# A post-norm layer on one core: scores in 32x32 tiles, |Kh| on ScalarE, Newton in one piece, new orders on every engine

## The reference, cut to what matters

```python
# x: (16, 256, 128); 16 heads of 8; window 128; FFN 128 -> 352 -> 128, fp4 in blocks of 16
g, v = x @ Wg.T + bg, x @ Wv.T + bv                       # per head
corr = dot(g_i, g_j) / (|g_i||g_j| + 1e-8), masked to j <= i and j >= i - 128
corr = (corr + 1) / 2
denom = mean_j(corr) + 0.5
fitness = 1 / (denom * sum_i(1 / denom))
attn = softmax(corr * fitness_i, masked with -1e10)
x = layernorm(x + (attn @ v) @ Wo.T + bo)
h = silu(q4(x) @ q4(Wgate).T) * (q4(x) @ q4(Wup).T)
x = layernorm(x + q4(h) @ q4(Wdown).T)
# q4: s = max|block| / 6; round x/s to the grid 0, .5, 1, 1.5, 2, 3, 4, 6; times s
```

## Time and profile before

| | |
|---|---|
| median of 3 runs | 390.52 us (386.58 to 390.61) |
| the profiled execution | 388.84 us, of which the span from first to last instruction is 387.0 us |
| mean granted TensorE clock | 0.944 of full |
| busy: PE, DVE, ACT, POOL | 329.3, 285.6, 223.8, 188.2 us |
| PE's matmul instructions | 2964, and as many weight loads |

### The profile page before, as it was taken

How to read it: one execution, slowest core, us unless ns; L and a number is a source line. 1 busy time by engine, 2 the same in 40 slices (tenths; PEclk the granted TensorE clock), 3 DMA queues, 4 the chain that set the end, 5 groups by cost and what they waited for, 6 DMA issues and landing times.

```text
span 387.0 us, 8906 instructions
## 1 busy us (share of the span) xinstructions
PE 329.3 (85%) x2964; PEld 196.2 (51%) x2964; DVE 285.6 (74%) x820; ACT 223.8 (58%) x499; POOL 188.2 (49%) x466
## 2 busy tenths in 40 slices
PE   6368878798899999999999999999998999967542
PEld 4234444454455565655565555555554556635331
DVE  1535356667879797979797979797979798886751
ACT  2034564566667776767676767777776777513210
POOL 7754033507274747374737373737373333541441
PEclk9999998899999999999999999999999999985655
DMA  4001000000010101010101010100000000000000
GB/s 117 27 1 29 14 2 3 27 2 29 0 30 3 42 1 42 0 46 1 42 0 45 1 43 2 43 0 30 3 30 0 29 3 27 15 0 14 15 14 19
DMA packets 12405, 7.64 MB, mean 20 GB/s; under 512 B 1026, under 2 KB 12356, under 8 KB 12356
## 3 DMA queue, kind: packets, MB, share of 16 engines
q1 hardware_dynamic: 12356, 7.03, 6.4%
HBM read 4.93 MB, written 2.10 MB: 18 GB/s over the span
## 4 chain that ended last, share of the span: by engine, by line
PE 30%; DVE 23%; POOL 20%; issue 17%; ACT 8%; POOLq 0%; ACTq 0%; DVEq 0%
PE OT L745 6%; PE S L722 5%; PE WA L871 4%; POOL nt L463 4%; PE S L726 3%; ACT Pm L561 3%; POOL rstd L496 3%; POOL nt L465 3%; POOL rn L470 3%; POOL nt L468 2%; DVE A L1274 2%; POOL B L510 2%; DVE xn L1166 2%; PE WB L784 2%; DVE h L1118 2%
## 5 line engine op out<-in xcount | busy, mean ns | idle before, releaser
L561 ACT ACTIVATE Pm<-S 128x384 f32<-128x384 f32 x256 | 111.7, 490 | 64.0 <-PE S L726 63.9
L722 PE MATMUL S<-mask,ident 128*128 128x384 f16 x256 | 65.8, 340 | 10.0 <-ACT Pm L561 7.8
L745 PE MATMUL OT<-Pm,gv 128*32 128x256 f32 (+1 forms) x1024 | 56.8, 341 | 0.0
L487 POOL TENSOR_TENSOR hq<-hm,hs 128x352 f32<-128x352 f32 x32 | 25.2, 789 | 63.8 <-DVE hm L1136 63.6
L726 PE MATMUL S<-BT,AT 32*128 32x256 f16 (+1 forms) x512 | 44.3, 252 | 0.0
L745 PEld LDWEIGHTS OT<-Pm,gv 128*32 128x32 f32 x1024 | 27.2, 111 | 21.4 <-issue 6.0
L726 PEld LDWEIGHTS S<-BT,AT 32*128 32x128 f16 x512 | 14.4, 93 | 43.0 <-issue 43.0
L722 PEld LDWEIGHTS S<-mask,ident 128*128 128x128 f16 x256 | 18.9, 99 | 33.7 <-issue 14.8
L840 PE MATMUL WD<-wdT,hqT 128*128 128x128 f32 (+1 forms) x192 | 29.5, 311 | 1.5 <-ACT hqT L614 1.5
L840 PEld LDWEIGHTS WD<-wdT,hqT 128*128 128x128 f32 (+1 forms) x192 | 26.3, 217 | 4.1 <-ACT hqT L614 2.2
L1112 DVE SCALAR_TENSOR_TENSOR hh<-th,WC 128x352 f32<-128x352 f32 x29 | 15.0, 518 | 17.7 <-ACT th L585 17.6
(11 more groups left out here) (160 smaller groups left out, 724.4 us busy)
## 6 DMA issues: line engine op xcount, KB each, us to landing
xT<-x_turned_dram SPq DMA_DIRECT2D x16, 128.0 KB, 2.2
x_res<-x_dram SPq DMA_DIRECT2D x16, 128.0 KB, 2.1
out_dram<-yo SPq DMA_DIRECT2D x16, 128.0 KB, 2.1
wf<-w_down_dram SPq DMA_DIRECT2D x1, 176.0 KB, 2.6
wgv<-wgv_dram SPq DMA_DIRECT2D x1, 128.0 KB
wf<-w_gate_dram SPq DMA_DIRECT2D x1, 128.0 KB, 2.2
wf<-w_up_dram SPq DMA_DIRECT2D x1, 128.0 KB, 2.2
woT<-wo_dram SPq DMA_DIRECT2D x1, 64.0 KB
```

Of the source, the lines that this page charges most:

```text
L487: pool.tensor_tensor(b3(hq[:, k, 0:I]), b3(hm[:, k]), bc(hs[:, k], QB), ALU.mult).then_inc(s_hq, 1)
L561: act.activation(Pm[:, group % PR, hd % 4, :], S[:, (H * x + hd) % 3, 0:SCW], ACT.Exp, scale=1.0 / ZS).then_inc(s_exp, 1)
L722: pe.matmul(S[:, bank, 0:SCW], ident16[:, :], mask16[:, :], start=True, stop=False)
L745: i = pe.matmul(OT[VP * g:VP * (g + 1), T - (q1 - q0):T], gv_flat[:, at:at + VP], Pm[:, (GROUPS * x + c) % PR, g, q0:q1], start=(kt == 0 a ...
```

## The change

- `scores`: the two L726 matmuls of a head become eight of at most 32 keys by 32 contraction rows. For keys 0 to 127 each tile of 32 keys covers 160 queries, for keys 128 to 255 it covers 128, 96, 64 and 32. The mask is added last, by four matmuls of a 32x32 identity with 3 x 32 columns of mask16. What lies outside of these is set to MASKED in PSUM once, by nine DVE memsets ahead of everything (awaited by the first exponential).
- `round_h`: ScalarE computes hu = |2^22 * hn - 4| (`step_of_h`), GpSimd's hrn is negated, and DVE rounds by two scalar_tensor_tensor: (max(hu, ROUND) + hn), (max(hu, ROUND) - hm).
- GpSimd: all three Newton steps in one piece at the start of its step, then B's high part, then rstd of layer norm 1; h/scale of both halves behind A's high part.
- DVE: for t >= 0 the three `gene_size` instructions stand between the fitness instructions, ahead of gate and up; gh ahead of the h scales; B's low part behind the maxima of h; x's quantising ahead of A's low part; at t < B the reciprocal and the attention stay inside `quant_x`.
- ACT: gsq and gv ahead of `values_out(t, 0)` and the exponentials of pair 6; `step_of_h` around the copy of B.

```diff
 scores(x, p)
-                for hd, bank in pair:
-                    pe.matmul(S[:, bank, 0:SCW], ident16[:, :], mask16[:, :], start=True, stop=False)
-                for kt, (q0, q1) in enumerate(((0, T), (T, SCW))):
+                for kt in range(NT):
                     for hd, bank in pair:
                         r, c = 32 * (hd % 4), hd // 4
-                        i = pe.matmul(S[:, bank, q0:q1], AT[r:r + 32, x % 2, c, kt * P:(kt + 1) * P],
-                                      BT[r:r + 32, x % 2, c, T - (q1 - q0):T], start=False, stop=(kt == 1))
-                        if kt == 1:
-                            i.then_inc(s_sc, 1)
+                        for k0 in range(0, P, KG):
+                            at, n = (k0, P + KG) if kt == 0 else (T + k0, P - k0)
+                            q = kt * P + k0
+                            pe.matmul(S[k0:k0 + KG, bank, at:at + n], AT[r:r + 32, x % 2, c, q:q + KG],
+                                      BT[r:r + 32, x % 2, c, q:q + n], start=(kt == 0), stop=False)
+                near = mask16[:, :].rearrange("p (b c) -> p b c", c=P)
+                for n, (hd, bank) in enumerate(pair):
+                    m = 32 * (hd % 4)
+                    for k0 in range(0, P, KG):
+                        i = pe.matmul(S[k0:k0 + KG, bank, 0:SCW].rearrange("p (b c) -> p b c", c=P)[:, :, k0:k0 + KG],
+                                      ident16[m:m + KG, m:m + KG], near[m:m + KG, :, m:m + KG],
+                                      start=False, stop=True)
+                    i.then_inc(s_sc, 1)
...
 GpSimd's step
                 if live(t + 2):
-                    newton(t + 2, (0, 1, 2) if t < 0 else (0,))
-                if live(t - 2) and t != B + 1:
-                    rstd(t - 2, mv1, ve1, rstd1, nm1, nb1, s_ln1, 5 * (t - 2) + 5, s_rs1)
+                    newton(t + 2)
...
                     pool.tensor_copy(B16[:, :, 0:3:2, :], twice(Bf)).then_inc(s_Bhi, 1)
-                if live(t + 2) and t >= 0:
-                    newton(t + 2, (1, 2))
-                if live(t - 3):
-                    h_over_scale(t - 3, 0)
+                if live(t - 2) and t != B + 1:
+                    rstd(t - 2, mv1, ve1, rstd1, nm1, nb1, s_ln1, 5 * (t - 2) + 5, s_rs1)
...
 ScalarE
+            def step_of_h(x, k):
+                act.wait_ge(s_hn, NT * x + k + 1)
+                act.activation(hu[:, k], hn[:, k], ACT.Abs, bias=off[:, :], scale=STEP).then_inc(s_hu, 1)
...
 round_h(x, k, step), two steps in place of four
+                dve.scalar_tensor_tensor(out=hm[:, k], in0=hu[:, k], scalar=ROUND, in1=hm[:, k] if step else hn[:, k],
+                                         op0=ALU.max, op1=op).then_inc(s_hr, 1)
...
 VectorE, ahead of everything
+            for k0 in range(0, P, KG):
+                for a, b in ((0, k0), (k0 + P + KG, T), (T, T + k0)):
+                    if a < b:
+                        dve.memset(S[k0:k0 + KG, :, a:b], MASKED).then_inc(s_far, 1)
```

More of the change, by code:

```diff
@@ L32 @@
 MASKED = -60000.0
+KG = 32
 ZS = 256.0
@@ L397, in _ @@
             pool.memset(onesf[:, :], 1.0).then_inc(c_pool, 1)
+            pool.memset(off[:, :], STEP_OFF).then_inc(s_off, 1)
             for n in range(2):
@@ L450, in bias_rows, with newton @@
                 pool.wait_ge(c_pool, 30)
-            def newton(x, steps):
+            def newton(x):
                 y0 = rn[:, :]
@@ L456, in newton @@
                 sd = seed[:, :].bitcast(F32)
-                for k in steps:
+                for k in range(3):
                     src = sd if k == 0 else y0
@@ L578, in apply_1 @@
                 need(act, s_ln2, 5 * (t - 2 - YR) + 1)
-                need(act, s_xq, 9 * (t - 2 - YR) + 5)
+                need(act, s_xq, 9 * (t - 2 - YR) + 4)
                 ln_apply(y, rstd1, nb1, y1[:, (t - 2) % YR], s_y1)
@@ L655, in _ @@
                                    WA[:, :].rearrange("p (q d) -> p q d", d=HD), ACT.Copy).then_inc(s_gvc, 1)
+                if live(t):
+                    values_out(t, 0)
+                exps(t, 6)
                 if live(t - 2):
@@ L1106, in residual_2, with low_B @@
                                   WD[:, 0:T].rearrange("p (n d) -> p n d", n=NT), ALU.add).then_inc(s_ln2, 1)
+            def low_B(x):
+                dve.wait_ge(s_Bhi, x + 1)
+                need(dve, s_B, x)
+                dve.tensor_tensor(B16[:, :, 1:4:2, :], twice(Bf), B16[:, :, 0:3:2, :], ALU.subtract).then_inc(s_Blo, 1)
             def gate(x, k):
@@ L1219, in _ @@
                     ln_aggr(t - 4, s_ln2, st2, mv2)
+                if t < 0 and live(t + 1):
+                    low_B(t + 1)
                 if live(t - 3):
@@ L1223, in _ @@
                     up(t - 3, 1)
[L1225 to L1232, removed]
                 if live(t + 2):
@@ L1237, in _ @@
                     need(dve, s_Alo, t + 2)
+                    need(dve, s_fit, 8 * (t + 2))
                     dve.tensor_tensor(gh[:, :, :],
@@ L1244, in _ @@
                 if live(t - 3):
+                    h_scale(t - 3, 0)
+                if t >= 0 and live(t + 1):
+                    low_B(t + 1)
+                if live(t - 3):
+                    h_scale(t - 3, 1)
                     h_scale(t - 3, 2)
-                if t == B:
+                if live(t - 2) and t < B:
+                    for step in range(4):
+                        quant_x(t - 2, step)
+                if live(t - 1):
                     dve.wait_ge(s_ob, t)
@@ L1249, in _ @@
                     dve.reciprocal(orec[:, :], o[:, :, HD]).then_inc(s_on, 1)
+                if live(t - 2) and t < B:
+                    quant_x(t - 2, 4)
+                if live(t - 1):
                     dve.wait_ge(s_on, t)
@@ L1252, in _ @@
                     dve.tensor_tensor(attn[:, :, :], o[:, :, 0:HD], bc(orec[:, :], HD), ALU.mult).then_inc(s_attn, 1)
[L1253 to L1275 removed]
+                if t == B:
+                    for step in range(5):
+                        quant_x(t - 2, step)
+                if live(t - 2) and t <= B:
+                    quant_x(t - 2, 5)
                     quant_x(t - 2, 6)
@@ L1280, in _ @@
                     down_weights()
+                if live(t + 2):
+                    dve.wait_ge(s_Ahi, t + 3)
+                    need(dve, s_A, t + 2)
+                    dve.tensor_tensor(A16[:, :, 2:4, :], twice(gh), A16[:, :, 0:2, :], ALU.subtract).then_inc(s_Alo, 1)
                 if live(t - 3):
                     round_h(t - 3, 0, 0)
-                    round_h(t - 3, 0, 1)
-                    round_h(t - 3, 0, 2)
                 if live(t - 4) and t != B + 1:
@@ L1325, in _ @@
                     gate(t - 2, 0)
-                if live(t + 3) and t != -2:
-                    gene_size(t + 3, 0)
-                if live(t - 2):
                     up(t - 2, 0)
-                if live(t + 3) and t != -2:
-                    gene_size(t + 3, 1)
-                    gene_size(t + 3, 2)
+                if t in (-3, -1):
+                    for k in range(3):
+                        gene_size(t + 3, k)
                 if t == -3:
```

79 lines of the change are left out of this document (31 added, 48 removed).

## The result

The changed kernel takes 364.2 us (median of 4 runs, 361.29 to 365.56), the one before 390.27 in the same comparison: a ratio of 0.935 (0.928 to 0.942). The forecast was 354, with 342 to 373 for the range. The profiled execution took 365.38, of which the span is 363.5, against 388.84 and 387.0 before. So 23.5 us of span went, where 36.1 were forecast.

A forecast was written before the change was run, and what follows sets the result against it. PE's work and a ring through the engines both held the 19.26 us period; the ring would bind at 17.1. Savings of 21.6, 4.5, 6.5, 1.0 and 2.5 took 388.84 to 352.7, plus 1.7 gave 354; range 342 to 373.

The forecast's parts named there:

- Up to 99.99 ... 6.5: Start up to the steady stretch: 1.8 for step 0, 3 for steps 1 and 2, 2 for the fill, less 0.3 memset.
- granted clock falling in the middle because PE now idles: One of the listed signs that would show the forecast wrong; no size given.
- The pair: Score matmuls of two heads on PE: from 0.70 us to 0.43, between bounds of 0.35 and 1.52.
- A: Rival on the scores: small matmuls cost 20 ns each rather than 7, pair 0.66, total 371; chance 0.15.
- B: Rival on the scores: tiles of one head run one after another at 0.056, total 469, slower; chance 0.05.
- PE's work: PE's work per steady period: 18.75 us of 19.26 before, 16.3 after the change.
- The ring: Dependency loop through the engines in each steady period: 17.1 us after, 4.1 of PE and ACT plus 13.0 of DVE.
- Rounding: Rounding h on DVE: from 3.42 us to 1.76 per period, saving 1.66.
- The seed: Newton's seed, three DVE instructions now ahead of rden: adds 0.65 us to the ring.
- rival C: GpSimd's rstd of layer norm 1 comes late: one us per period, ring 18.1, total 364 to 366; chance 0.12.
- D: Rival on ACT: Abs needs another function table, four loads of 1.283 us, some 400 us; chance 0.04.
- Two further steps, last pairs, tail: Savings after the ten steady periods: 4.5 us for two steps, 1.0 for last pairs and rounding, 2.5 for the tail.

The follow-up runs named there:

- e1_warm: The changed kernel with idle-time matmuls ahead of pairs in steps 0 and 1 and ahead of step 2's turn of the weights: 356.93 us, ratio 0.919.
- e3_tiles_only: The kernel before with only the new 32x32 scores and their nine memsets: 401.26 us, ratio 1.033.
- e4_old_scores: The changed kernel with the old scores everywhere: 376.86 us, ratio 0.970.
- e7: e1_warm with the three gene_size (seed) instructions right behind rden instead of between the fitness instructions: 358.94 us.
- e9: e1_warm with layer norm 1's rstd between Newton steps two and three, its apply ahead of pair 2's exponentials, h maxima ahead of gh: 371.70 us, ratio 0.958.
- e10_fill_all: e1_warm with more idle-time matmuls, from the start through step 0 and in the gaps of the last steps: 352.68 us, ratio 0.908.
- e6: e1_warm with GpSimd's old order (rstd and B's high part after Newton step one) and the seed behind gate and up: 424.03 us, ratio 1.093.
- e8_tiles_filled: e3_tiles_only with twelve idle-time matmuls of 256 columns ahead of the turn of xm: 386.94 us, ratio 0.996.

## Why the prediction was right or wrong

The direction, the range and most of the mechanism held; the time was 10 us too low.

- **The step that failed: "Up to 99.99 ... 6.5".** I counted what pairs and DVE save and took the clock for granted, though the kernel before already had short falls in this stage. A list of what would show me wrong had "granted clock falling in the middle because PE now idles", but no rival and no term had it, and it came not in the middle but at the start. Measured: -0.7, so 7.2 of the 12.6 us are missing here. By stage: ahead of step 0 forecast 1.7 (five pairs less the memset), measured 0.1; step 0 forecast 1.8, measured -1.35; steps 1 and 2 forecast 3, measured 0.54. The last two are the clock's, as e1_warm shows: with the clock held up it has 2.8 and 6.1 there, the fall of the kernel before included. The first is not. There the new orders, for which I had put no term into the fill, cost 2.8 us (13.22 us in e3_tiles_only, 16.06 with them), more than the 2 that the pairs gave.
- **The pair.** Forecast 0.43 with two changes of form in it. From first start to the next matmul it is 0.28, but the change into the 32x32 form now stands ahead of it, in the distance of its predecessor: from the second half of gate/up to the pair it is 0.69 (195.22 to 195.91), where the kernel e4_old_scores has 0.59. In the forecast's terms the pair is 0.38, near the low bound of 0.35. 24 starts at 7 ns were nearly right, and there was luck in it: the 7 ns came from 0.42 - 0.40, two rounded listings. Rivals A and B fall. The Trainium skill (TensorEngine Tiling, Instruction Overhead) has an overhead of about 60 cycles per matmul, however few its columns; as an estimate from that page a pair would be 0.78, and the trace does not agree with it.
- **PE's work.** "18.75 of 19.26": e4_old_scores shows 18.46. "16.3" after: 17.41 less 1.67 of waits, 15.7. As forecast, it does not bind.
- **The ring.** Forecast 17.1, measured 17.4. From the sum of rden to hh 4.00 (196.51 - 192.51) against 4.1; DVE's part 13.4 against 13.0. The wait for y1 is 0.44 rather than 0.2. Rounding takes 2.14 by distances (187.56 to 187.99, 188.32 to 188.76, 189.15 to 190.01, 190.17 to 190.58) rather than 1.76, since the third instruction takes 0.93, beside GpSimd's hq at 188.92. The seed is 0.1 cheaper, 0.56. And e7 and e9 show that the ring is not alone: with the seed behind rden, a loop through Newton, rstd and y1 holds the period at 17.4, and with rstd early DVE's own instructions hold it at 17.8. Ten periods lost 2.6 us against the forecast by the longer DVE part.
- **rstd late (rival C).** By its place right, by size not: rstd and nb are ready 7.0 us after rden (forecast 6.6). The wait for y1 is 0.24 us longer than in my sum, not 1, and at most 0.1 of it is rstd's.
- **Abs.** 0.60 us, not 0.47: 0.26 us per period more on ACT, which has room. There is one table load, at the start, as before, so D falls. The Trainium skill (ScalarE: Activation LUTs, Table sets) has Abs in every set, and the source view agrees with it:

```profile
L661 ACT ACT_TABLE_LOAD  x1: 1283/1283/1283, 0.8 to 0.8; - x1
```

- **Two further steps, last pairs, tail.** 5.2 against 8.0. In the further steps I had let the saving per period grow to 2.4; it was 1.4. In the tail two roundings at 0.64 (3.42 - 2.14, halved) would make 1.3 of the 1.65, as an estimate from the steady rows; at my 0.7 to 1 each, with followers, I had 2.5.
- **Slips in the sums.** B and D are 0.09 together, not 0.08, and A's 371 lacks the 1.7 us that the forecast adds at its end. Neither changes the range.

What stays open: what holds the start at 89 us in e10_fill_all beside step 2, where the clock is still at 0.80, and how e6's loss divides between the ring and the clock. No run has the new rounding or the new orders alone in the kernel before, and none has the new orders with B's low part ahead of gh in the fill only, which the 2.8 us ask for.

## What to carry to other kernels

When a change makes TensorE's work lighter, ask at once what fills the gap: if the engine that bounds the loop was not made faster by as much, the gap may cost the clock, and then the lighter kernel is the slower one (401 us for the tiles alone, 389 before them). Look at the granted clock stage by stage, in the start above all, before a saving is written down for it; where it falls, a few useless matmuls in the idle time can pay: 7 us here, and 11 to 12 with all the places filled. An order that is right for the steady stretch can be wrong for the fill, so price it there too: 2.8 us here. And changes that come as a bundle are priced as a bundle. Without the tiles the changed kernel lost 13 us; with four-instruction rounding, or with Newton and the seed late, e1_warm lost 39 and 67, the fall of the clock included. Each of the last two is more than the whole change brings.

## What the runs showed of the hardware that was not expected

- 32x32 tiles start 7 ns apart, weight loads included: 16 of them, with up to 160 moving columns each, in 0.11 us. I had this figure only for tiles of 128 rows.
- With the ring unchanged, a PE that is idle for 2.5 us once a period has its clock fall in every period (0.92 over eight periods in e3_tiles_only), and 12 useless matmuls in that gap take 1.5 us off each period (e8_tiles_filled).
- At the very start the row of granted clocks can say 1.00 while the matmuls run at the lower level: the four gene matmuls at 40.67 are listed with 2.08 us, those at 100.75 with 1.03.
- DVE instructions of the same shape differ by a factor of up to three, in these rows with what GpSimd does beside them: hs 0.18 or, beside the cast of A, 0.59; the rounding step 0.52 or, beside hq, 0.93.
